# Softmax score and maximum matmuls as four 32-column tiles, and the wide attention's 192 channels as 128 plus a doubled 64

## The reference, cut to what matters

```
q = q * cos + _rotate_half(q) * sin
k = k * cos + _rotate_half(k) * sin
attn = jnp.einsum('bhnd,bhmd->bhnm', q * scale, k)
attn = jax.nn.softmax(attn, axis=-1)
out = jnp.einsum('bhnm,bhmd->bhnd', attn, v)
```

```
att = jnp.einsum('bqd,bkd->bqk', q, k) * nd ** (-0.5)      # nd = 192
att = jax.nn.softmax(att, axis=-1)
y = jnp.einsum('bqk,bkd->bqd', att, v)
y = jnp.transpose(y, (0, 2, 1)).reshape(B, S, nd)
return jnp.einsum('bsd,ed->bse', y, Wc) + bc
```

## Time and profile before

| | before |
|---|---|
| median of 3 runs | 8088.04 us (8078.62 to 8089.96) |
| the profiled execution | 8075.42 us |
| span of its trace | 8073.9 us |
| PE busy | 7029.6 us (87%) |
| VectorE busy | 4767.7 us (59%) |
| ScalarE busy | 3186.2 us (39%) |
| GpSimd busy | 2308.3 us (29%) |

### The profile page before, as it was taken

One profiled execution on the slowest core, in us unless ns is written; L12 is line 12 of the kernel. 1 busy time (PEld: TensorE's weight loads), 2 busy tenths in 40 slices (PEclk: granted clock), 3 DMA queues, 4 the chain that ended last, 5 costly groups with the idle time before them and its releaser, 6 DMA issues. The chain is left out here.

```text
span 8073.9 us, 195165 instructions
## 1 busy us (share of the span) xinstructions
PE 7029.6 (87%) x68587; PEld 3990.2 (49%) x68587; DVE 4767.7 (59%) x7714; ACT 3186.2 (39%) x5336; POOL 2308.3 (29%) x2558
## 2 busy tenths in 40 slices
PE   6699999999999577499999998089788999999977
PEld 4233333333333455166666677057554555555546
DVE  6777777777775320222223224411278999999986
ACT  2166666666667124122222222011244454444432
POOL 0011111111111100000000001300128999999971
PEclk8699999999999788699999996589899999999986
DMA  4211111111110522501000002121282111111123
GB/s 119 65 34 35 31 29 34 34 34 33 33 28 25 139 73 55 146 2 27 1 27 1 18 1 89 66 63 52 71 257 66 38 36 37 38 37 37 37 63 101
DMA packets 414316, 426.09 MB, mean 53 GB/s; under 512 B 76199, under 2 KB 386635, under 8 KB 408590
## 3 DMA queue, kind: packets, MB, share of 16 engines
q1 hardware_dynamic: 331790, 339.52, 14.9%
q0 software_dynamic: 62400, 59.16, 2.9%
q10 hardware_dynamic: 19712, 21.53, 0.8%
HBM read 253.37 MB, written 166.55 MB: 52 GB/s over the span
## 5 line engine op out<-in xcount | busy, mean ns | idle before, releaser
L624 DVE TENSOR_REDUCE softmax_part_max<-softmax_ring 128x1 f32<-128x512 f32 (+1 forms) x2880 | 1727.1, 634 | 493.8 <-PE softmax_ring L534 462.4
L664 ACT ACTIVATE softmax_probs<-softmax_scores 128x768 f32<-128x768 f32 x1728 | 1399.2, 811 | 884.0 <-PE softmax_scores L553 845.1
L2441 POOL TENSOR_TENSOR retention_decayed<-retention_third,retention_decay_table 128x384 f32<-128x384 f32 x1728 | 1691.6, 1008 | 102.9 <-ACT retention_third L2463 98.8
L2422 DVE TENSOR_TENSOR retention_decayed<-retention_scores,retention_decay_table 128x768 f32<-128x768 f32 x1728 | 1655.0, 958 | 89.9 <-PE retention_scores L2383 57.5
L2383 PE MATMUL retention_scores<-retention_q_half,retention_k_piece 96*32 96x384 bf16 x20736 | 1196.5, 325 | 35.2 <-DMA retention_v_piece<-ret_v 28.9
L534 PE MATMUL softmax_ring<-softmax_k_next,softmax_q_next 96*128 96x512 bf16 (+1 forms) x2880 | 1086.5, 379 | 140.9 <-DVE softmax_part_max L624 48.7
L2395 PE MATMUL retention_sums<-retention_decayed,retention_v_piece 128*32 128x288 f32 x13824 | 1192.3, 407 | 3.2 <-POOL retention_decayed L2441 0.6
L2463 ACT COPY retention_third<-retention_scores 128x384 f32<-128x384 f32 x1728 | 828.1, 479 | 890.9 <-PE retention_scores L2383 890.9
L565 PE MATMUL softmax_sums<-softmax_probs,softmax_v_piece 128*32 128x192 f32 x13824 | 928.7, 343 | 0.6 <-ACT softmax_result L653 0.5
L2383 PEld LDWEIGHTS retention_scores<-retention_q_half,retention_k_piece 96*32 96x32 bf16 x20736 | 652.6, 95 | 492.2 <-DVE retention_decayed L2422 41.4
L553 PE MATMUL softmax_scores<-softmax_q_third,softmax_k_piece 99*128 99x384 bf16 x3456 | 871.2, 334 | 5.0 <-ACT softmax_probs L664 5.0
(11 more groups left out here) (299 smaller groups left out, 6497.3 us busy)
## 6 DMA issues: line engine op xcount, KB each, us to landing
ret_v<-ret_proj_values SPq DMA_DIRECT2D x8, 1728.0 KB, 8.5
retention_v_piece<-ret_v SPq DMA_DIRECT2D x144, 96.0 KB
softmax_q_third<-rope_q SPq DMA_DIRECT2D x192, 54.0 KB
softmax_q_next<-rope_q POOLq DMA_DIRECT2D x64, 162.0 KB, 4.1
softmax_k_piece<-rope_k SPq DMA_DIRECT2D x192, 54.0 KB
softmax_k_next<-rope_k POOLq DMA_DIRECT2D x64, 162.0 KB, 5.6
ret_q<-ret_proj_parts SPq DMA_DIRECT2D x48, 216.0 KB
ret_k<-ret_proj_parts SPq DMA_DIRECT2D x48, 216.0 KB
```

The lines of the kernel that those rows point to most:

```text
L624: nc.vector.reduce_max(part_max[:, j, c:c + 1], ring[m % 2][:, 0:CHUNKS[c][1]], axis=X)\
L664: nc.scalar.activation(probs[n % 4][:, :].rearrange("p (c q) -> p c q", c=2), scores[n % 2][:, :, 0:QC], ACT.Exp, scale=scale).then_inc(ex ...
L2422: nc.vector.tensor_tensor(weights[n % 4][:, 0:2 * QC].rearrange("p (c q) -> p c q", c=2), scores[n % 2][:, 0:2, 0:QC], table[:, table_at(n ...
L2441: nc.gpsimd.tensor_tensor(weights[n % 4][:, 2 * QC:HALF], third[n % 3][:, :], table[:, at:at + QC], ALU.mult)\
```

## The change

In the softmax stage each chunk matmul becomes four, one for each 32 queries, and each of the two score matmuls of a step becomes four, one for each 32 keys. Every one writes its own 32 partitions of the same bank. The semaphores stay, on the last of the four.

In the wide attention q and k are laid as 128 channels and 64 channels, and the 64 are stored twice, in partitions 0 to 63 and 64 to 127. The second part's projection weight is loaded twice side by side for that, and the projection's matmuls and copies now have 128 partitions instead of 96. A tile's scores are five matmuls over 128 rows (`long_part`) followed by five over 64 rows (`short_parts`), which take the upper and the lower copy in turn. The long parts of the next tile are placed between the groups of transposes of the current one. The weights come in by seven DMAs in place of five.

```
-                return nc.tensor.matmul(ring[m % 2][:, 0:width], q_next[i][:, j * P:(j + 1) * P],
-                                        k_next[i][:, at:at + width], start=True, stop=True).then_inc(ring_full, 1)
+                for g in range(4):
+                    rows = j * P + 32 * g
+                    last = nc.tensor.matmul(ring[m % 2][32 * g:32 * g + 32, 0:width], q_next[i][:, rows:rows + 32],
+                                            k_next[i][:, at:at + width], start=True, stop=True)
+                last.then_inc(ring_full, 1)
...
-                    last = nc.tensor.matmul(scores[n % 2][:, c, 0:QC],
-                                            k_piece[t // PT][:, t % PT * P:(t % PT + 1) * P],
-                                            q_third[third][:, c * QC:(c + 1) * QC], start=True, stop=True)
+                    for g in range(4):
+                        at = t % PT * P + 32 * g
+                        last = nc.tensor.matmul(scores[n % 2][32 * g:32 * g + 32, c, 0:QC], k_piece[t // PT][:, at:at + 32],
+                                                q_third[third][:, c * QC:(c + 1) * QC], start=True, stop=True)
...
-        wqk, wv = sb("wqk", [HC + 1, 2, 2, 2, HC], F32), sb("wv", [HC + 1, 2, C], F32)
+        wqk, wv = sb("wqk", [HC + 1, 2, 2, 2, P], F32), sb("wv", [HC + 1, 2, C], F32)
...
-        qk_t = sb("qk_t", [HC, 2, 2, N], F32)
+        qk_t = sb("qk_t", [P, 2, 2, N], F32)
...
+            channels = w_qk.rearrange("p h i f c -> p (h i) (f c)")
+            for part, at, of in [(0, 0, channels[:, :, 0:P]), (1, 0, channels[:, :, P:C]), (1, OVER, channels[:, :, P:C])]:
+                sp.dma_start(wqk[:, :, :, part, at:at + (of.shape[2])].rearrange("p h i c -> p (h i) c"), of).then_inc(consts_in, 16)
...
-            def score(b, i):
-
-                pe.wait_ge(exped, b * TILES + i)
-                for at, width in CHUNKS:
-                    for f in range(2):
-                        last = nc.tensor.matmul(scores[:, at:at + width], qk_t[:, 0, f, i * P:(i + 1) * P],
-                                                qk_t[:, 1, f, at:at + width], start=(f == 0), stop=(f == 1))
+            def long_part(i, c):
+                at, width = CHUNKS[c]
+                nc.tensor.matmul(scores[:, at:at + width], qk_t[:, 0, 0, i * P:(i + 1) * P], qk_t[:, 1, 0, at:at + width],
+                                 start=True, stop=False)
+
+            def short_parts(i):
+                for c, (at, width) in enumerate(CHUNKS):
+                    rows = slice(c % 2 * OVER, c % 2 * OVER + OVER)
+                    last = nc.tensor.matmul(scores[:, at:at + width], qk_t[rows, 0, 1, i * P:(i + 1) * P],
+                                            qk_t[rows, 1, 1, at:at + width], start=False, stop=True)
                 last.then_inc(scored, 1)
...
+            def turn_and_score(b, i):
                 pe.wait_ge(exped, b * TILES + i + 1)
...
+                turn(b, i, 0)
+                for g in range(1, NG):
+                    turn(b, i, g)
+                    if i + 1 < TILES:
+                        long_part(i + 1, g - 1)
+                if i + 1 < TILES:
+                    long_part(i + 1, len(CHUNKS) - 1)
+                    short_parts(i + 1)
...
                 for i in range(TILES):
-                    turn(b, i)
-                    if i + 1 < TILES:
-                        score(b, i + 1)
+                    turn_and_score(b, i)
                     value(b, i)
```

More of the change, by code:

```diff
@@ L1309, in wide_attention @@
         OUTS = 2 * (TILES // 3)
+        OVER = C - P
         def bank(n):
@@ L1318, in _ @@
         def _(sp):
-            for to, of in [(identity[:, :], ident), (wqk[:, :, :, :, :], w_qk), (wv[:, :, :], w_v),
+            for to, of in [(identity[:, :], ident), (wv[:, :, :], w_v),
                            (wo[:, :, :], w_out), (bo[:, :], out_bias.partition_broadcast(HC))]:
                 sp.dma_start(to, of).then_inc(consts_in, 16)
+            channels = w_qk.rearrange("p h i f c -> p (h i) (f c)")
+            for part, at, of in [(0, 0, channels[:, :, 0:P]), (1, 0, channels[:, :, P:C]), (1, OVER, channels[:, :, P:C])]:
+                sp.dma_start(wqk[:, :, :, part, at:at + (of.shape[2])].rearrange("p h i c -> p (h i) c"), of).then_inc(consts_in, 16)
             ln.load(sp, 0, x[0, :, :], first=True)
@@ L1336, in _ @@
             ln.set_ones(pool)
-            pool.wait_ge(consts_in, 80)
+            pool.wait_ge(consts_in, 112)
             with pool.Fori(0, images) as b:
@@ L1354, in projections @@
                         chunk = slice(c * ln.W, (c + 1) * ln.W)
-                        nc.tensor.matmul(bank(n)[0:HC, 0:ln.W], wqk[:, 0, i, half, :], ln.xn[:, 0, chunk], start=True, stop=False)
-                        nc.tensor.matmul(bank(n)[0:HC, 0:ln.W], wqk[0:HC, 1, i, half, :], ln.xn[0:HC, 1, chunk],
+                        nc.tensor.matmul(bank(n)[:, 0:ln.W], wqk[:, 0, i, half, :], ln.xn[:, 0, chunk], start=True, stop=False)
+                        nc.tensor.matmul(bank(n)[:, 0:ln.W], wqk[0:HC, 1, i, half, :], ln.xn[0:HC, 1, chunk],
                                          start=False, stop=True).then_inc(proj_full, 1)
@@ L1364, in projections @@
                         last.then_inc(proj_full, 1)
-            def score(b, i):
-                pe.wait_ge(exped, b * TILES + i)
-                for at, width in CHUNKS:
-                    for f in range(2):
-                        last = nc.tensor.matmul(scores[:, at:at + width], qk_t[:, 0, f, i * P:(i + 1) * P],
-                                                qk_t[:, 1, f, at:at + width], start=(f == 0), stop=(f == 1))
-                last.then_inc(scored, 1)
-            def turn(b, i):
-                pe.wait_ge(exped, b * TILES + i + 1)
[L1377 to L1389, removed]
@@ new lines, in turn @@
+            def turn(b, i, g):
+                t0, n = TGROUPS[g]
+                pe.wait_ge(pt_act, (b * TILES + i) * len(ON_ACT) + (g // 2 if g % 2 == 0 else 0))
+                pe.wait_ge(pt_dve, (b * TILES + i) * len(ON_DVE) + (g // 2 if g % 2 else 0))
+                for k in range(n):
+                    last = nc.tensor.transpose(ring[g % 2][:, k * P:(k + 1) * P],
+                                               probs[i % 2][:, (t0 + k) * P:(t0 + k + 1) * P], identity[:, :])
+                last.then_inc(pt_full, 1)
@@ L1399, in value @@
                 last.then_inc(valued, 1)
-            pe.wait_ge(consts_in, 80)
+            pe.wait_ge(consts_in, 112)
             pe.wait_ge(ln.ones_row, 1)
@@ L1410, in _ @@
                 pe.wait_ge(proj_free, (b + 1) * USES)
-                score(b, 0)
+                for c in range(len(CHUNKS)):
+                    long_part(0, c)
+                short_parts(0)
                 for i in range(TILES):
-                    turn(b, i)
-                    if i + 1 < TILES:
-                        score(b, i + 1)
+                    turn_and_score(b, i)
                     value(b, i)
@@ L1441, in _ @@
                         half, c = divmod(rest, ln.CHUNKS)
-                        nc.scalar.copy(qk_t[:, i, half, c * ln.W:(c + 1) * ln.W], bank(n)[0:HC, 0:ln.W]).then_inc(proj_free, 1)
+                        nc.scalar.copy(qk_t[:, i, half, c * ln.W:(c + 1) * ln.W], bank(n)[:, 0:ln.W]).then_inc(proj_free, 1)
                     else:
```

## The result

The changed kernel takes 7705.46 us in the median of 4 runs (7699.02 to 7713.58), the kernel before 8084.59 us in 4 runs. The ratio is 0.9532 (95% interval 0.9515 to 0.9548), 379 us less. Its trace spans 7704.4 us for 8073.9. From the first to the last PE record the softmax stage went from 2333 to 2118 us, the wide attention from 1500 to 1347 us. These 215 and 153 us are nearly the whole of the 369.5 us between the two spans. The 379 us are the difference of the medians.

The account below looks back on a forecast made before the run. PE was taken to bound the softmax, with VectorE close behind. Savings of 245 us (softmax) and 166 us (wide attention), 411 us, from 8088 us gave 7680 us (rounded up), range 7600 to 7770.

Parts of the forecast that it names:

- the cycles: Softmax: three steps with five chunks take 3.22 us, 0.44 less, saving 7.9 us a head, 245 us over 31 heads.
- the last heads: Softmax: the head without maxima beside it was left at no saving (0 to 4 us).
- The cost of a change of width: Softmax: PE loses 0.14 us behind the value and 0.10 us ahead of it, 0.24 us a step.
- The handover: Softmax: PE and VectorE share two banks, so three steps take 3.31 or 3.14 us, depending on the empty half step's place.
- the other 2.1 us are the waits around the transpose, which I leave: Softmax: of a 68.03 us head, 65.9 us are steps; the remaining 2.1 us of transpose waits stay unchanged.
- The loop's 4.21 us jump stays: Softmax: PE's idle time of 4.21 us at the loop's turn, with no releaser, remains unchanged.
- I charge nothing: Softmax: a head's load and matmul pairs grow from 630 to 1224, but instruction supply holds, at no added time.
- Issue: Softmax rivals: retention's mean per pair, 7763 us, chance 0.12; instructions set the pace, 8387 us (8232 at 62 ns), 0.05.
- The wide attention: Wide attention: a tile takes 14.12 us, 2.35 less; 160 us for 68 tiles, with four first tiles 166 us.
- the first tiles, counted at 6: Wide attention: four first tiles save 1.5 us each.
- The 2.5 us for the short parts: Wide attention: a tile's paired short parts taken at 2.25 us, plus 0.10 us for each of two changes of shape.

Follow-up runs that it names:

- the two halves alone: Against the kernel before, only the chunks made of 32-column matmuls: 8161.66 us; only the scores made of 32-column matmuls: 8410.2 us.
- halved maxima: VectorE takes each maximum over half of a chunk only: 7534.83 us on the changed kernel, 8035.07 us on the kernel before.
- even chunks: The changed kernel with six chunks of 384 keys in place of four of 512 and one of 256, AHEAD 28 for 23: 7650.99 us.

## Why the prediction was right

**The total.** 7680 us was forecast and 7705 measured. Of the 411 us of saving that were forecast, 379 came. Both parts saved less than was forecast. Within the softmax some errors cancel: the cycles and the last heads saved more, the stops took more back.

**The cost of a change of width** was 0.24 us a step, read as 0.14 and 0.10. After, the same distances are 0.32 and 0.23 us, as read from the retention. Of the two halves alone, one kept the 108 changes of a head and left the stage where it was (2339 us for 2333). The other made 180 changes and cost 7 us a head. The Trainium skill, page "TensorEngine Tiling (Array Packing)", section "Key Properties", says that a change of tiling mode drains the engine. The trace agrees in that each change costs about 0.1 us. It does not tell a drain from a weight load that is no longer hidden. Before, the score's weight load began together with its matmul at 1150.97, and after, it began 0.16 us ahead (986.13 for 986.29).

**The handover** was followed as 3.31 and 3.14 us for three steps. In the trace after, the exponential three steps on starts 3.27 us later in one part of a head and 3.11 us in another, for 3.66 before (timeline of ScalarE, the changed kernel):

```profile
971.65 0.81 ACT L668 ACTIVATE softmax_probs<-softmax_scores 128x768 f32<-128x768 f32 x1 [0.39 <-PE softmax_scores L558]
...
974.92 0.81 ACT L668 ACTIVATE softmax_probs<-softmax_scores 128x768 f32<-128x768 f32 x1 [0.39 <-PE softmax_scores L558]
...
984.72 0.81 ACT L668 ACTIVATE softmax_probs<-softmax_scores 128x768 f32<-128x768 f32 x1 [0.18 <-PE softmax_scores L558]
...
987.83 0.81 ACT L668 ACTIVATE softmax_probs<-softmax_scores 128x768 f32<-128x768 f32 x1 [0.17 <-PE softmax_scores L558]
```

The saving in the cycles was therefore right, even a little low (8.5 us a head where 7.9 stood).

**The terms that were mis-sized in the softmax.** The head periods fell by 6.7 us in the mean, not 7.9, and 31 x 6.7 = 209 us in place of 245. An undisturbed head fell by 68.03 - 60.15 = 7.88 us, as forecast. In it "the other 2.1 us are the waits around the transpose, which I leave" was somewhat low, which the cycles made up for: VectorE's row maximum and the splitting of the maxima used to lie in its spare time and now add to the head (two steps with the transpose take 2.1 us more than others, for 1.7 before).

What is missing are stops in which PE waits for nothing that the profile shows. "The loop's 4.21 us jump stays" was right (2.7 to 4.8 us now, 2.8 to 4.3 before), but a second stop of 1.5 to 2.7 us follows each turn. In ten of the fifteen heads without a turn there is a third, of 0.3 to 1.5 us, some 60 us behind the turn:

```profile
1216.36 0.36 PE L569 MATMUL softmax_sums<-softmax_probs,softmax_v_piece 128*32 128x192 f32 x3 [1.14 <-issue]
```

"I charge nothing" for supply was thus too little, behind the turn and in straight code. That it is the supply of instructions fits the instruction queue, which moved 44 packets in two passes of the loop (900 to 1160 us) for 26 before (900 to 1190 us), but no run tried it by itself.

The heads from the last transpose on, which have no maxima beside them, were "left at nothing (0 to 4 us)". They saved 7.5 us (55.2 for 62.6), and so the stage saved 215 us and not 209.

**Issue** did not bind. The Trainium skill, page "TensorE: Matmul & The Clock Gate", section "Step-by-step: what each phase is for", gives 62 ns for each matmul with the hardware decoder off. With halved maxima a pair took 46 ns, so that case was not in force here.

**The wide attention** saved 153 us for 166 forecast. The tile came out at 14.23 us for 14.12. The pairs overlap fully, and two changes of shape cost the 0.10 us each that were taken. The excess lies in the values, 5.95 us (3306.31 to 3312.26) where 5.85 was taken: their first record holds the second back by 0.27 us, the later ones follow 0.16 us apart. The exponentials stayed covered, as PE goes from values to transposes without idling. 68 x 2.24 = 152 us is nearly all of it, which leaves 1 us for the first tiles, counted at 6. The 2.5 us for the short parts, worked out from the Trainium skill, page "TensorE: Matmul & The Clock Gate", section "Measured speedup vs the span model", was too high for the 2.34 us measured. The page gives its 3.07 times for 32 rows and 512 columns and does not name bf16 there.

## What to carry to other kernels

Look for the one matmul whose shape differs from its neighbours: the cost is in the change, so narrowing all neighbours pays, and narrowing some of them pays nothing or costs. When PE speeds up and hands work over through two banks, follow bank by bank which side waits. The uneven chunk and the empty slot are where it loses, and even chunks gave 54 us back. Do not take the wait of a weight load that runs ahead for a bound: halve the other side's work and look at the time. When many more instructions are issued, look at the turns of long loops and at stages that were not touched.

## What the runs showed of the hardware

Two 64-row groups of the array work at once in fp32: ten records in 2.34 us paired and 4.06 us unpaired. Four 32-column groups cost the same as one 128-column matmul (0.33 us from a score of eight narrow matmuls to the next record, as from one of two wide ones), and a pair of load and matmul took 46 ns over a whole head. PE's granted clock stayed at its 1.2 GHz level for 3 to 58 us of full records behind a turn when every chunk changed the width. Three effects at loops were not expected: the second stop behind a turn (1.5 to 2.7 us), ScalarE's own turn showing once PE's is gone (4.26 us), and a small loop whose instructions are fetched again (157 us) though its code is the same.
